# A causal attention stage rewritten: two batches in the 128 rows, the mask as a product in the score bank, eight slots instead of two

## The reference, cut to what matters

```python
h = layernorm(x)
q, k, v = rope(rms(h)*ln1 @ wq.T), rope(rms(h)*ln1 @ wk.T), rms(h)*ln1 @ wv.T   # 4 heads of 16; 2 of k, v
scores = where(causal, q @ k.T / 4, -1e30)
y = h + (softmax(scores) @ v) @ wo.T          # x + y is the stream for later
flat = rms(y) * ln2                           # handed to the experts
probs = softmax(flat @ router_w.T)            # 8 experts; the two largest, renormalised, are handed on
```

## Time and profile before

| | |
|---|---|
| median of 3 runs | 9736.86 us (9732.4 to 9858.74) |
| profiled execution | 9755.44 us, its span 9753.6 us |
| mean granted TensorE clock | 0.674 |
| PE busy | 8114.1 us (83%) |
| PE weight loads | 5958.8 us (61%) |
| VectorE busy | 4793.1 us (49%) |
| ScalarE busy | 2652.9 us (27%) |
| GpSimd busy | 794.8 us (8%) |
| attention 1, from its first to its last instruction | 2141.6 to 3984.2 us |

### The profile page before, as it was taken

How to read it: one execution, slowest core, us unless ns; L and a number is a source line. 1 busy time by engine, 2 the same in 40 slices (tenths; PEclk the granted TensorE clock), 3 DMA queues, 4 the chain that set the end, 5 groups by cost and what they waited for, 6 DMA issues and landing times. The chain is left out here.

```text
span 9753.6 us, 133122 instructions
## 1 busy us (share of the span) xinstructions
PE 8114.1 (83%) x40361; PEld 5958.8 (61%) x40361; DVE 4793.1 (49%) x11789; ACT 2652.9 (27%) x6187; POOL 794.8 (8%) x804
## 2 busy tenths in 40 slices
PE   4399567988778778798999787888888898878888
PEld 4266454546556555565777555777777777756666
DVE  1455344545555555344444565455555455545555
ACT  3234100001111111243222113444444444423333
POOL 0022111000000000121000000000000000000000
PEclk9977555555555555798555555677777677769999
DMA  0100111111111111332000110000000000000000
GB/s 8 26 21 21 26 40 34 24 24 9 9 9 10 9 9 9 61 81 58 15 15 15 23 27 15 5 5 5 5 5 5 5 3 5 5 15 13 11 11 10
DMA packets 637014, 172.15 MB, mean 18 GB/s; under 512 B 612740, under 2 KB 632244, under 8 KB 636726
## 3 DMA queue, kind: packets, MB, share of 16 engines
q1 hardware_dynamic: 636854, 170.45, 10.0%
HBM read 124.98 MB, written 45.40 MB: 17 GB/s over the span
## 5 line engine op out<-in xcount | busy, mean ns | idle before, releaser
L2951 DVE TENSOR_TENSOR att_SM<-att_pS,att_mask 125x498 f32<-125x498 f32 x512 | 346.1, 676 | 952.3 <-PE att_pS L2768 889.1
L2768 PE MATMUL att_pS<-att_kT,att_qT 64*125 64x249 f32 x2048 | 749.0, 534 | 0.9 <-ACT att_V L2848 0.9
L2797 PEld LDWEIGHTS att_pO<-att_V,att_PTr 124*125 124x125 f32 (+1 forms) x4096 | 700.4, 248 | 64.9 <-issue 22.0
L2797 PE MATMUL att_pO<-att_V,att_PTr 124*125 124x64 f32 (+1 forms) x4096 | 670.4, 322 | 0.0
L2782 PE MATMUL att_pP<-att_ident,att_P 124*125 124x124 f32 (+1 forms) x2048 | 484.2, 375 | 187.9 <-ACT att_P L2866 187.9
L2782 PEld LDWEIGHTS att_pP<-att_ident,att_P 124*125 124x125 f32 (+1 forms) x2048 | 364.9, 253 | 421.4 <-issue 421.4
L2866 ACT ACTIVATE att_P<-att_SM,att_nb 125x249 f32<-125x249 f32 x1024 | 503.2, 494 | 359.6 <-DVE att_nb L2953 359.6
L2859 ACT ACTIVATE att_PTr<-att_pP 125x498 f32<-125x498 f32 x512 | 300.0, 586 | 927.9 <-PE att_pP L2782 927.9
L2768 PEld LDWEIGHTS att_pS<-att_kT,att_qT 64*125 64x125 f32 x2048 | 435.3, 254 | 108.2 <-issue 20.4
L3095 PEld LDWEIGHTS sw_pY<-sw_w,sw_hT 128*125 128x125 f32 x4096 | 466.1, 189 | 3.7
L3095 PE MATMUL sw_pY<-sw_w,sw_hT 128*125 128x64 f32 x4096 | 461.4, 271 | 0.0
(11 more groups left out here) (512 smaller groups left out, 16742.5 us busy)
## 6 DMA issues: line engine op xcount, KB each, us to landing
moe_share<-mixing SPq DMA_DIRECT2D x64, 498.0 KB
att_F<-h_stream SPq DMA_DIRECT2D x192, 62.5 KB
att_X<-h_stream SPq DMA_DIRECT2D x192, 62.5 KB
ffn_w<-in_w1b SPq DMA_DIRECT2D x128, 32.5 KB
ffn_w<-in_L_ffn_W SPq DMA_DIRECT2D x128, 32.0 KB
h_stream<-att_H SPq DMA_DIRECT2D x64, 62.5 KB
ffn_F<-h_stream SPq DMA_DIRECT2D x64, 62.5 KB
ffn_X<-h_stream SPq DMA_DIRECT2D x64, 62.5 KB
```

The source lines that it names most:

```text
L2768: ins = pe.matmul(pS[:, s % 2, t * T:t * T + T], qT[r:r + D, u, hp, b, t * OFF:t * OFF + PT], kT[r:r + D, u, hp, b, :], start=True, stop=True,
L2797: ins = pe.matmul(pO[:, t, hd * D:(hd + 1) * D], PTr[0:ROWS[kt], s % 2, kt, t * OFF:t * OFF + PT], V[0:ROWS[kt], u, 2 * kt + b, hd * D:(hd ...
L2951: link(v.tensor_tensor(SM[:, s % 2, :, :], pS[:, s % 2, 0:2 * T].rearrange("p (t n) -> p t n", t=2), mask[:, u, b:4:2, :], ALU.add))
```

## The change

Attention 1 is rewritten with `waves`, generalised to a longer period: eight parts (`pre, proj, front, main, post, ends, last, mixed`) of eight different pairs are in work in a slot of 8 steps, buffers are numbered modulo 4. Two batches share the 128 rows of every transpose and projection; weights come block-diagonal or doubled from the host; `ln1` and `ln2` are scales of the copy after a transpose. LayerNorm and RMS norm become one (`ways=2`: two exponents from one sum of squares). The mask is written into the score bank by a bf16 product of the identity with the mask (374 columns), and the fp32 scores are added to it; maximum and exponential then read the bank itself. GpSimd takes the centring, the scales, the sum of the two rotation terms, the residual and the comparison of the experts. Ranking uses one difference and one comparison with `ties`. Value products have 32 columns of weights in four column groups, batch 0 in step 0 and batch 1 in step 1. The mixing weights are transposed and stored by rows in one DMA. The expert stage loads the tokens with one DMA instead of two.

```diff
-def waves(engine, parts, steps, last=None):
+def waves(engine, parts, steps, period=2):
...
-    with engine.Fori(0, whole) as j:
-        for u in range(2):
+    with engine.Fori(0, whole) as j:
+        for u in range(period):
+            slot(j * period + (depth - 1 + u), (depth - 1 + u) % period)
...
+    STEPS, PERIOD, WAVES = 8, 4, 12
...
+                def project(k, n, u):
+                    for j in range(2):
+                        for b in range(2):
+                            r = slice(b * C, (b + 1) * C)
+                            ins = pe.matmul(pQ[:, b, j * T:(j + 1) * T], wqk[r, 2 * k + j, :], xT[r, u % 2, :],
+                                            start=True, stop=True)
...
+                def by_query(n, u, s):
...
+                    pe.wait_ge(*max_ready.after(n, s - 2))
+                    pe.matmul(bank[:, 0:LOW], ident16[0:PT, 0:PT], mask16[:, 0, :], start=True, stop=True)
+                    pe.matmul(bank[:, 0:PT], qT[r:r + D, u % 2, b, 0:PT], kT[r:r + D, u, b, 0:PT], start=False,
+                              stop=True, tile_position=(r, 0), skip_group_check=True)
+                    pe.matmul(bank[:, PT:LOW], qT[r:r + D, u % 2, b, OFF:T], kT[r:r + D, u, b, :], start=False,
+                              stop=True, tile_position=(r, 0), skip_group_check=True).then_inc(*s_done.one())
...
+                def by_key(n, u, s):
+                    b, r = s // H, 32 * ((s + 2) % H)
+                    bank = pS[:, s % 2, :]
+                    if s % H == 0:
+                        pe.wait_ge(*qm_ready.after(n, b))
+                    pe.wait_ge(*exp_ready.after(n, s - 2))
+                    pe.matmul(bank[:, 0:LOW], ident16[0:PT, 0:PT], mask16[:, 1, :], start=True, stop=True)
...
+                def values(n, u, b):
+                    for hd in range(H):
+                        pe.matmul(pO[32 * hd:32 * hd + 32, b * T:(b + 1) * T],
+                                  V[0:OFF, u, 0, b * KV + hd // 2, :], EX[0:OFF, u % 2, b, hd, 0:T],
+                                  start=True, stop=True)
+                    for hd in range(H):
+                        ins = pe.matmul(pO[32 * hd:32 * hd + 32, b * T + OFF:(b + 1) * T],
+                                        V[:, u, 1, b * KV + hd // 2, :], EX[:, u % 2, b, hd, T:LOW],
+                                        start=False, stop=True, skip_group_check=True)
...
+                def post(n, u, step):
+                    if step == 0:
...
+                        values(n, u, 0)
+                    if step == 1:
+                        values(n, u, 1).then_inc(*o_done.one())
...
+                waves(pe, (nothing, proj, front, main, post, ends, last, mixed), STEPS, PERIOD)
...
+                def main(n, u, step):
+                    a.wait_ge(*st_done.after(n, step))
+                    a.activation(EX[:, u % 2, step // H, (step + 2) % H, :], pS[:, step % 2, 0:LOW], ACT.Exp,
+                                 scale=D ** -0.5).then_inc(*exp_ready.one())
...
+                    v.wait_ge(*s_done.after(n, step))
+                    v.tensor_reduce(M[:, 0, b, hd, D:DV], bank[:, 0:PT], AX.X, ALU.max, negate=True)
+                    v.tensor_reduce(M[:, 1, b, hd, D:DV], bank[:, PT:LOW], AX.X, ALU.max, negate=True).then_inc(
+                        *max_ready.one())
+                    if step == 6:
+                        add_max(n, u, 0)
...
-                    for b in range(2):
...
-                        sp.dma_start(x[rows, u, :], bass.AP(src.tensor, src.offset + b * T, [[2 * T, C], [1, T]])
-                                     ).then_inc(*x_loaded.one(u))
+                    sp.dma_start(x[:, u, :], src.rearrange("o c t -> (o c) t")).then_inc(*x_loaded.one(u))
```

More of the change, by code:

```diff
@@ new lines, in _ @@
+                for n in range(2):
+                    ahead(n, n)
+                    keep(n, n)
+                for n in range(2, 6):
+                    ahead(n, n % 2)
+                for n in range(2):
+                    ahead(n + 6, n)
+                    store(n, n)
+                    keep(n + 2, n)
+                with sp.Fori(0, (PAIRS - 8) // 2) as j:
+                    for u in range(2):
+                        n = j * 2 + (2 + u)
+                        ahead(n + 6, u)
+                        store(n, u)
+                        keep(n + 2, u)
+                        store_mix(n - 2, u)
@@ L1760, in _, with last @@
+                def last(n, u, step):
+                    if step == 3:
+                        w = lg[:, :, :]
+                        other, own = bcm(w, 2, E), bc(w, E)
+                        g.wait_ge(*l_exp.after(n))
+                        g.wait_ge(*rank_ready.before(n))
+                        g.tensor_tensor(over[:, :, :, :], other, own, ALU.subtract).then_inc(*compared.one())
+                waves(g, (pre, proj, nothing, nothing, nothing, ends, last, nothing), STEPS, PERIOD)
             @block.tensor
@@ L1761, in _ @@
             def _(pe):
[L1762 to L1782 removed]
+                pe.wait_ge(*const_loaded.after(0))
@@ new lines, in last @@
+                def last(n, u, step):
+                    if step == 1:
+                        pe.wait_ge(*flT_ready.after(n))
+                        pe.wait_ge(*l_shifted.before(n))
+                        pe.wait_ge(*x2_ready.after(upto(n + 1)))
+                        st.held(pe)
+                        for t in range(2):
+                            ins = pe.matmul(pX[0:PT, t * 2 * E:(t + 1) * 2 * E], flT[:, u % 2, t * OFF:t * OFF + PT],
+                                            wr[:, :], start=True, stop=True)
+                        ins.then_inc(*l_done.one())
@@ L1961, in link, with ends, last @@
+                def ends(n, u, step):
+                    if step == 1:
+                        tail.spread(v, n, 1e-6)
+                def last(n, u, step):
                     def link(ins):
@@ L2021, in split_weights @@
+                waves(v, (pre, proj, front, main, post, ends, last, nothing), STEPS, PERIOD)
 def split_weights(v, w, rest, hm, mh, lh, chain):
```

760 lines of the change are left out of this document (421 added, 339 removed).

## The result

| us | before | after |
|---|---|---|
| median, same chip, four runs each | 9751.08 (9732.4 to 9858.74) | 9385.2 (9365.33 to 9512.97) |
| profiled execution | 9755.44 | 9365.33, its span 9363.3 |
| mean granted TensorE clock | 0.674 | 0.683 |
| attention 1, first to last instruction | 1842.6 | 1472.0 |
| all other stages | | 19.7 less |

The ratio is 0.960 with a 95% interval of 0.951 to 0.969; it leaves out the changed kernel's slow execution of 9512.97 us (clock 0.671), which the median of four holds. The forecast was 9410 us. Between the two profiled executions 390 us went where 327 were forecast.

What follows compares the result with a forecast made beforehand. PE at half clock, 44.5 us work plus 11.3 waiting a pair, bounds attention 1; waits go, work becomes 46.5, less 1.0 for clock: 32 x 45.5 + 60 = 1516 us, kernel 9410 us, range 9285 to 9498 (9280 to 9580 with part of the waits rival).

Steps and rivals of the forecast that it cites:

- Score steps: Attention 1, 8 steps a pair, each two score sets, two mask products and their changes: 4.20 us a step, 33.6 a pair.
- The rival of the changes: Changes of array form around mask products above 0.61 us each eat the gain; at 0.65, kernel about 9830 us; chance 0.07.
- Projections: Attention 1, eight 249-column products in two steps, costed from attention 0's 1.96 us for four: 3.9 us a pair.
- Values: Attention 1 value products, two batches 2.5 us plus 0.6 for two changes: 3.1 us a pair, against 10.1 before.
- All else: Other full-array work in attention 1 (V, logits, `wo`, transposes): 28 passes of 0.21, 5.9 us a pair.
- The clock: Attention 1 mostly at half clock, with short full-clock stretches now and then, taken as 1.0 us a pair saved.
- The place named for it: Longest full-array run, projection of step 5 with `wo` and a mask of step 6, expected to release full clock now and then.
- Start and end: Attention 1's time outside its 32 pairs, eight slots deep instead of two: taken as 60 us, ends 50 and 85.
- The rule on weight loads: Skill: loads overlap only across row groups, making 48 score passes some 8 us a pair dearer; prediction kept 1.25 a set.
- The clock rival: PE without waits releases the clock in attention 1, as in attention 0 (0.73): stage 1126, kernel 9020 us; chance 0.13.
- the 3.9 us wait: PE's wait in the old attention 1, read as the second norm before its transpose, a norm said to be gone.
- side-by-side sets: A step's two score sets running at once on different rows would save 10.0 us a pair; mask between said to forbid it.

Runs made afterwards that it cites:

- masks first: Changed kernel with both mask products of a step issued before both score sets, which then run on different rows; 8881 us, attention 1 959.5 us.
- values together: Changed kernel with the value products of both batches in step 0 again instead of steps 0 and 1; 9325 us, attention 1 1423.0 us.
- `wo` early: Changed kernel with the `wo` product in step 5, right behind the transpose whose copy it needs, instead of step 6; 9397 us.
- Taking one link off: Kernel before, with both causal masks of attention 1 left out; 9588 us, attention 1 1767.5 us.
- drawing one back: Changed kernel with `wo` in step 5 instead of step 6; 9397 us, attention 1 1515.4 us.
- mask on VectorE: Changed kernel with both masks added by VectorE and the mask products removed; 8708 us, attention 1 893.8 us.
- masks first with values together: Changed kernel with both mask products ahead of both score sets and both batches' values in step 0; 8852 us, attention 1 921.7 us.

## Why the prediction was right, and by which terms it was off

The mechanism held. PE's work stayed where it was (45.40 us a pair at half clock; before, 56.3 less the 11.3 of waiting is 45.0), its waits vanished, the clock stayed at half but for short stretches, and the range held the time. Term by term, in us a pair:

- **Score steps**, forecast 33.6: 8 x 4.08 = 32.6. The passes and the 0.30 of one change were exact (1.54 a set). Mask and the other change, forecast at 0.31 + 0.24, measured 0.50 together. The rival of the changes needed more than 0.61 for each; they measured 0.19 and 0.29.
- **Projections**, forecast 3.9: L1863 to L1993 is 1.96 us (2922.61 to 2924.58 and 2968.01 to 2969.97), twice: 3.9.
- **Values**, forecast 3.1: 2 x 1.41 = 2.8. **All else**, forecast 5.9, is by difference 45.4 - 32.6 - 3.9 - 2.8 = 6.1.
- **The clock**, forecast as 1.0 saved: 45.4 - 44.9 = 0.5. Six stretches of full clock stand between 2240 and 3570 us, most some 270 us apart. The place named for it is right in the one looked at. The projection and `wo` fill the full array from 2968.01 to 2970.98, the mask follows, and the clock is up:

```profile
2967.80:2971.20 3.40, 3.40 (x14) 2.21 (x13) 1.73 (x4) 0.00 (x0) 0.00 (x0) 0.50 0.23 53
2971.20:2974.60 3.40, 3.40 (x17) 2.25 (x16) 1.33 (x5) 0.48 (x1) 1.07 (x1) 0.98 0.00 0
```

- Together the pair in the middle is 44.9 where 45.5 was forecast: 1.0 + 0.3 less and 0.2 more of work, 0.5 less clock saved. By first to last over 31 it is 43.8, below the announced 45 to 47.
- **Start and end**, forecast 60: 1472 - 32 x 44.9 = 34 us. This is the term that was most off, and by how it was taken. The 57 us of the kernel before came from a pair averaged over all copies, the short last ones with it (by its middle, 56.3, it would be 42); the forecast added 60, a term taken in that way, to pairs summed from the work of a full one.
- **Sum**: the pairs give 18 us more than forecast, start and end 26 more, and the other stages 20 that were not forecast (327 + 18 + 26 + 20 is the 390 measured, within rounding).

**The rule on weight loads.** Four passes and one change of form in 1.54 us leave no room for a paid load at each pass (with the prediction's 0.16 a load, an estimate behind which no row stands, it would be near 2.0). The rule of the Trainium skill ("TensorE: Matmul & The Clock Gate", Part 3) does not hold between products on the same rows here. On different rows the trace agrees with it: the two sets of "masks first" start 0.01 us apart.

**The clock rival.** PE busy 98% of the stage did not release the clock (0.51), so a fed PE is not enough, as said. Runs with the same products in another order moved it: with values together, where 3.6 us of full-array products stood ahead of a rise, it was 0.52, with masks first 0.60, and with `wo` early 0.50. The Trainium skill (same page, Part 1) says that activity of the array releases the throttle; if a busy PE is taken for activity, the trace does not agree (98% busy, 0.51).

**What the prediction had wrong.** It called the 3.9 us wait of the earlier trace rows the second norm and said that this norm is gone. The row names `att_fl`, the norm of the result, and that norm is still there. Its wait went since it now lies whole steps ahead of its transpose. The front's second norm, which is indeed gone, was a small wait before. The conclusion stood because the argument about whole steps covers both. Other stages were to stay within 0.3%: attention 0 moved by -1.5%, attention 3 by -0.9%, the switch stage by +1.2%, retention 1 and attention 2 by less than 0.1%.

It also noted that side-by-side sets would save 8 x 1.25 = 10.0 us. It took the mask between them as forbidding it and did not see that it was within reach by order alone. With the change of form saved too, it was 14.2. This was the largest thing missed in the case, more than the whole gain forecast.

VectorE was forecast under 21 us a pair and has 13.0, ScalarE under 9 and has 7.1, GpSimd 9.1 and has 8.5. None limits, so in the new form taking the mask off VectorE buys nothing: 26.0 us a pair with it there, 43.8 with it on PE in this order.

## What to carry to other kernels

When a busy engine's own work and its waits for single links add up to the time of a pair, spread the chain over more steps. Taking one link off brought out the next; drawing one back cost 0.86 us a pair. A small product of another array form between two sets on different rows can cost far more than its columns: here 0.31 us of its own, and 1.77 us a step for where the two of a step stood. Count what stands on both sides of it, put such products together, or give them to an engine with room. Cost PE's work and its clock apart, on stretches that lie wholly at one clock: here order alone, with the same products, made 1.4 of 1.7 us a pair. And take a loop's time from its middle; the pairs at the end are shorter.

## What the runs showed that was not expected

**An unedited stage moved by 4%.** Attention 3, the same code in all kernels, took from 2613 to 2722 us, at a clock of 0.74 to 0.71. The shortest and the longest:

```profile
4954.30:7567.60 2613.30, 2322.16 (x11264) 1837.99 (x11264) 1368.04 (x3339) 1179.93 (x3247) 180.03 (x224) 0.74 0.02 5
```
```profile
4991.70:7713.80 2722.10, 2411.56 (x11264) 1902.41 (x11264) 1369.51 (x3339) 1181.42 (x3247) 180.10 (x224) 0.71 0.03 6
```

The first is of the mask on VectorE, the second of masks first with values together. VectorE's and ScalarE's busy times are the same to 0.2%; what differs is TensorE's clock and its busy time. Stages that stay at half clock all through (attention 2, retention 1) never moved by more than 0.3%. What in a kernel decides it was not tried. Until it is known, 100 us of difference between two kernels' totals can come from a stage that neither edits, and an edit should be judged by its own stage's span too.

**Order alone moved the clock.** Nearly the same PE work a pair (45.4 us at half clock, 45.1 with values together) took 44.9, 43.2 and, with one link's wait, 46.3 us in the middle of the stage, only by where the values and `wo` stood.
